# Causal attention with split-precision scores: the row sums of the last three key tiles of a chunk move from TensorE to VectorE, masks are merged, and visits to the values hold up to eight key tiles

## The chip, the cores and the metric

One core of one Trainium2 chip runs the whole program. The metric is the device time of that core in microseconds (us). The kernel before took 3632.71 us, the median of three runs (3631.72 to 3634.29).

## What is computed

A causal attention with grouped heads, a residual and a layer norm, then a linear layer with eight low-rank experts and a second layer norm. The change touches the attention alone:

```
q = (x @ wq).reshape(b, s, 32, 32)        # b = 2, s = 2048, x: [2, 2048, 1024]
k, v = (x @ wk), (x @ wv)                 # 8 key/value heads of 32, each shared by 4 query heads
scores = einsum('bihd,bjhd->bhij', q, k) * 32 ** -0.5
scores = where(causal, scores, min)
attn = softmax(scores, axis=-1)
out = einsum('bhij,bjhd->bihd', attn, v) @ wo
```

## The kernel before

The program has three stages, one behind the other: `project_qkv` (to about 550 us), `attend` (to about 2690 us) and `feed_forward`. The change lies in `attend`.

`attend` works on 16 groups, one for each batch and key/value head, with the group's four query heads side by side. For a group it does two things on TensorE (PE), interleaved:

- **The maxima.** Scores are computed with queries on the partitions, in *items* of up to 512 columns (`item`, L532), into a ring of three banks `qm`. VectorE (DVE) reduces each item to one maximum per row (L674) and so frees its bank. Diagonal items get a causal mask by a small matmul with the identity (L535). There are 140 such items in a group, and four transposes of the maxima (L524). They are computed half a group ahead of their use, and a table places two items (transposes counted) behind each step: 144 on 72 steps.
- **The exponentials and the values.** Scores are computed again with keys on the partitions (`scores`, L556, and L550 for the last tile), 128 keys by 256 queries by four heads in a pair of banks `km` (there are two pairs). ScalarE (ACT) takes the exponential (L637, and L634 for half a tile) into a ring of 18 tiles `probs`. Queries come in eight *chunks* of 256, numbered 0 to 7; chunk c has 2c + 2 key tiles, each a *step*, 72 in all. The last tile of a chunk is half masked away, and only 128 of its queries are computed.

Steps come in *slots* of at most five (`MOST = 5`), 18 slots in a group. Behind the scores of a slot TensorE makes a *visit* to the values (`values`, L566) for the slot before it: for each key tile four matmuls, one for each head in its own quarter of the array, multiply `probs` by `v` into `p2_o`. The profile counts each of these fp32 matmuls as two instructions, so that a tile shows as x8.

The denominators are the sums of `probs` over the keys. GpSimd (POOL) adds the first 2c - 1 tiles of chunks 2 to 7 into `psums` (L499 for the first pair, L503 for the rest), and one call of `weighted` multiplies the sum by ones. The last three tiles of these chunks, and all of chunks 0 and 1, are multiplied by ones on TensorE, tile by tile (`weighted(ones, probs)`, L566 too). In the last group POOL takes only c + 1 tiles of chunks 3 to 7 (`LAST_SUMS`). At the end of a chunk TensorE waits for POOL's last sum (`added`), and ACT copies `p2_o` out (L617).

Every engine works through its own list in order. SyncE issues all transfers. TensorE waits for ACT before it reuses a pair of `km`, for DVE before it reuses one of the three `qm` banks, for ACT's last exponential of a slot at the start of the visit to it, and for POOL at a chunk's end. ACT waits, before it overwrites a tile of the ring, for the visit and for POOL's sum that used it.

Of the kernel before, what the change touches and what calls it, by code (L numbers as in the profile page):

```python
# [5 lines left out]
F32 = mybir.dt.float32  # L6
# [8 lines left out]
P = 128  # L15
# [219 lines left out]
def attend(nc, sem, q_hi, q_lo, k_hi, k_lo, v_d, aT_d, den_d):  # L235
# [11 lines left out]
    MOST = 5  # L247
# [8 lines left out]
    PB = 18  # L256
    assert NS % PB == 0

# [4 lines left out]
    class Sums:  # L263

        def __init__(self, pooled):
            self.pooled = pooled
            self.adds_before = [sum(max(0, m - 1) for m in pooled[:c]) for c in range(NC + 1)]
            self.chunks = [sum(m > 0 for m in pooled[:c]) for c in range(NC + 1)]
# [4 lines left out]

        def adds_through(self, s):
# [5 lines left out]
    NADD, NCHUNK = SUMS.adds_before[NC], SUMS.chunks[NC]  # L280
# [59 lines left out]
    with ctx:  # L340
# [11 lines left out]
        psums = [sb(f"p2_psums{i}", [P, REP, CQ], F32) for i in range(2)]  # L352
        part_max = [sb(f"p2_part_max{c}", [P, REP, SUB, c + 1], F32) for c in range(NK)]
# [20 lines left out]
        added = sem("p2_added")  # L374
        chunk_done = sem("p2_chunk_done")
# [102 lines left out]
        def _(pool):  # L478
# [12 lines left out]
            def group(n, plan):  # L491
                for c in range(NC):
                    sums = psums[c % 2]
                    for t in range(1, plan.pooled[c]):
                        s = FIRST_STEP[c] + t
                        pool.wait_ge(exp_done, n * NS + s + 1)
                        if t == 1:
                            at_least(pool, chunk_done, n * NCHUNK + max(0, plan.chunks[c] - 1))
                            pool.tensor_tensor(sums[:, :, :], probs[(s - 1) % PB][:, :, :], probs[s % PB][:, :, :],  # L499
                                               ALU.add).then_inc(added, 1)  # L500
                        else:
                            pool.wait_ge(added, n * NADD + plan.adds_through(s) - 1)
                            pool.tensor_tensor(sums[:, :, :], sums[:, :, :], probs[s % PB][:, :, :],  # L503
                                               ALU.add).then_inc(added, 1)
# [7 lines left out]
        def _(pe):  # L512
            def item(m, par, i):
# [28 lines left out]
            def scores(n, par, s):  # L542
# [5 lines left out]
                if t == 2 * c + 1:  # L548
                    four = pair[:, 0, :].rearrange("p (h q) -> p h q", h=REP)
                    pe.matmul(four, keys, q_st[par][0:ROWS + 1, c // 2, :, q0 + P:q0 + CQ], start=True, stop=False)  # L550
                    last = pe.matmul(four, ident_bf[:, :], mask_k[:, :].unsqueeze(1).to_broadcast([P, REP, P]),
                                     start=False, stop=True)
                else:
                    for x in range(2):
                        two = pair[:, x, :].rearrange("p (h q) -> p h q", h=2)
                        last = pe.matmul(two, keys, q_st[par][0:ROWS + 1, c // 2, 2 * x:2 * x + 2, q0:q0 + CQ],  # L556
                                         start=True, stop=t < 2 * c)
                        if t == 2 * c:
                            last = pe.matmul(two[:, :, 0:P], ident_bf[:, :],
                                             mask_k[:, :].unsqueeze(1).to_broadcast([P, 2, P]), start=False, stop=True)  # L560
# [9 lines left out]
            def values(n, par, sl, plan):  # L570
# [7 lines left out]
                for s in steps:  # L578
                    t = STEPS[s][1]
                    last = weighted(v[par][:, t, :], probs[s % PB], 0, offset(s), t == 0)  # L580
                    if not plan.on_pool(s):
                        last = weighted(ones[:, :], probs[s % PB], CQ, offset(s), False)
                last.then_inc(slot_done, 1)
                if t == 2 * c + 1 and plan.pooled[c]:
                    pe.wait_ge(added, n * NADD + plan.adds_before[c + 1])
                    weighted(ones[:, :], psums[c % 2], CQ, 0, False).then_inc(chunk_done, 1)
# [23 lines left out]
        def _(act):  # L610
            def output(n, c, plan):
                if plan.pooled[c]:
# [13 lines left out]
            def exps(n, s, plan):  # L626
# [3 lines left out]
                if plan.on_pool(u % NS):  # L630
                    at_least(act, added, (n if u >= 0 else n - 1) * NADD + plan.adds_through(u % NS))
                act.wait_ge(scored, n * NS + s + 1)
                if offset(s):
                    act.activation(probs[s % PB][:, :, P:CQ], km[s % 2][:, 0, :].rearrange("p (h q) -> p h q", h=REP),  # L634
                                   ACT.Exp, scale=SCALE).then_inc(exp_done, 1)
                else:
                    act.activation(probs[s % PB][:, :, :].rearrange("p h q -> p (h q)"),  # L637
# [28 lines left out]
        def _(dve):  # L666
# [13 lines left out]
            def group(n, placed):  # L680
                for items in placed:
                    for ahead, i in items:
                        item(n + ahead, i)
# [8 lines left out]
            group(NG - 1, CLOSING)  # L692
# [746 lines left out]
```

## Time and profile before

| what | value |
|---|---|
| median of three runs | 3632.71 us |
| the profiled execution's own time | 3631.32 us |
| its span in the profile | 3629.2 us |
| mean granted TensorE clock | 0.986 |
| PE, PEld (weight loads), DVE, ACT, POOL busy | 97%, 68%, 53%, 41%, 43% |

The profile is of one execution; times in it count from the span's start. A matmul's start is measured, its end is modelled and overlaps the next one, so the pace of TensorE is read from starts and not from its busy share. A row of the timeline merges equal neighbours; the bracket at its end gives the engine's idle time before it, and who ended it.

### The profile page before, as it was taken

What the parts mean: (1) busy time and instruction counts of PE and PEld (TensorE: products, weight loads), DVE (VectorE), ACT (ScalarE), POOL (GpSimd) and SP (SyncE); (2) the same over time, 40 slices, a digit from 0 to 9 for tenths busy, and PEclk for the clock granted to TensorE, in tenths of its full rate; (3) what the DMA queues carried; (4) which work ended last, traced back from release to release, by engine and by line L of the source; (5) the groups of instructions that cost most, each with busy time, mean ns of one, the idle gap of its engine ahead of it and who ended that gap; (6) DMA issues with size and microseconds to landing.
All of it is one profiled execution on the core that took longest, in us unless ns stands there. A gap on an engine that the chain in (4) does not pass through costs nothing. (4 is left out here: it accounts for less than half of the span.)

```text
span 3629.2 us, 64158 instructions
## 1 busy us (share of the span) xinstructions
PE 3517.4 (97%) x26506; PEld 2460.0 (68%) x26506; DVE 1927.5 (53%) x3577; ACT 1491.4 (41%) x1839; POOL 1559.7 (43%) x672
## 2 busy tenths in 40 slices
PE   8999998999999999999999999999969999999999
PEld 7888885555565565665665556556537888888887
DVE  3121217666666666666666666666615666642223
ACT  3111112555555555555555555555542222221111
POOL 0000002767867777787786787787530000000000
PEclk9999997999999999999999999999989999999999
DMA  6343325021111111111112111110027777755553
GB/s 209 119 128 113 112 86 114 23 50 48 34 41 48 39 34 50 47 31 44 48 31 50 48 33 41 48 38 9 12 81 199 231 228 225 213 187 178 175 181 129
DMA packets 248227, 340.74 MB, mean 94 GB/s; under 512 B 55440, under 2 KB 150288, under 8 KB 247952
## 3 DMA queue, kind: packets, MB, share of 16 engines
q1 hardware_dynamic: 247952, 336.87, 31.6%
q8 instruction: 198, 3.24, 0.4%
q14 instruction: 77, 0.63, 0.1%
HBM read 203.08 MB, written 133.17 MB: 93 GB/s over the span
## 5 line engine op out<-in xcount | busy, mean ns | idle before, releaser
L674 DVE TENSOR_REDUCE p_part_max<-p_qm 128x1 f32<-128x512 f32 (+3 forms) x2240 | 1357.1, 669 | 716.5 <-PE p_qm L532 442.9
L503 POOL TENSOR_TENSOR p_psums<-p_psums,p_probs 128x1024 f32<-128x1024 f32 x560 | 1331.4, 2378 | 82.0 <-ACT p_probs L637 2.2
L637 ACT ACTIVATE p_probs<-p_km 128x1024 f32<-128x1024 f32 x1024 | 1032.0, 1024 | 542.5 <-PE p_km L556 438.1
L532 PE MATMUL p_qm<-p_k_st,p_q_st 96*128 96x512 f32 (+3 forms) x2560 | 916.4, 421 | 14.7 <-DMA p_q_st<-q_hi 10.7
L556 PE MATMUL p_km<-p_q_st,p_k_st 97*128 97x512 f32 x2048 | 714.5, 428 | 9.5 <-ACT p_probs L637 7.2
L532 PEld LDWEIGHTS p_qm<-p_k_st,p_q_st 96*128 96x128 f32 x2560 | 495.4, 196 | 230.8 <-DVE p_part_max L674 162.8
L566 PE MATMUL p_o<-p_probs,p_v 128*32 128x256 f32 (+1 forms) x9216 | 581.8, 371 | 0.0
L556 PEld LDWEIGHTS p_km<-p_q_st,p_k_st 97*128 97x128 f32 x2048 | 355.2, 192 | 156.3 <-issue 110.7
L499 POOL TENSOR_TENSOR p_psums<-p_probs 128x1024 f32<-128x1024 f32 x95 | 226.2, 2381 | 501.0 <-ACT p_probs L637 501.0
L566 PEld LDWEIGHTS p_o<-p_probs,p_v 128*32 128x32 f32 x9216 | 270.9, 110 | 213.6 <-issue 58.8
L41 PE MATMUL p_acc<-p_xT_hi,p_w_hi 128*128 128x512 f32 x640 | 250.1, 391 | 9.5 <-DVE p_w_lo L226 9.5
L42 PE MATMUL p_acc<-p_xT_lo,p_w_hi 128*128 128x512 f32 x640 | 249.8, 390 | 0.0
L43 PE MATMUL p_acc<-p_xT_hi,p_w_lo 128*128 128x512 f32 x640 | 249.7, 390 | 0.0
L214 DVE TENSOR_TENSOR p_out_lo<-p_acc,p_out_hi 128x512 fp32r<-128x512 f32 x80 | 55.3, 692 | 348.4 <-ACT p_out_hi L188 348.3
L41 PE MATMUL p_acc<-p_wo_hi,p_a_hi 128*128 128x512 f32 x512 | 209.1, 408 | 31.5 <-DVE p_a_lo L1219 31.5
L32 POOL MEMSET p_ident<- 128x128 f32 x2 | 0.4, 204 | 553.2 <-POOLq L63 542.0
L535 PE MATMUL p_qm<-p_mask_q,p_ident_bf 128*128 128x128 bf16 x1024 | 233.1, 236 | 0.0
L617 ACT ACTIVATE p_o_raw<-p_o 128x512 f32<-128x512 f32 x128 | 76.6, 599 | 367.5 <-PE p_o L566 367.5
L188 ACT ACTIVATE p_out_hi<-p_acc 128x512 fp32r<-128x512 f32 x80 | 47.9, 598 | 422.0 <-PE p_acc L43 408.5
L566 PE MATMUL p_o<-p_probs,p_ones 128*32 128x256 f32 (+1 forms) x3216 | 220.9, 346 | 0.0
L43 PE MATMUL p_acc<-p_wo_hi,p_a_lo 128*128 128x512 f32 x512 | 203.2, 397 | 0.0
L42 PE MATMUL p_acc<-p_wo_lo,p_a_hi 128*128 128x512 f32 x512 | 202.4, 395 | 0.0
(152 smaller groups left out, 3958.3 us busy)
## 6 DMA issues: line engine op xcount, KB each, us to landing
p_q_st<-q_hi SPq DMA_DIRECT2D x128, 256.0 KB, 4.7
p_x_raw<-in_xT SPq DMA_DIRECT2D x64, 256.0 KB, 3.5
q_hi<-p_out_hi SPq DMA_DIRECT2D x64, 256.0 KB, 2.0
q_lo<-p_out_lo SPq DMA_DIRECT2D x64, 256.0 KB, 2.3
p_q_st<-q_lo SPq DMA_DIRECT2D x64, 256.0 KB, 4.4
attended_T<-p_o_raw SPq DMA_DIRECT2D x128, 128.0 KB
p_a_raw<-attended_T SPq DMA_DIRECT2D x32, 512.0 KB, 4.9
p_recip<-reciprocals SPq DMA_DIRECT2D x128, 128.0 KB, 6.7
```

Source lines behind the costliest of these rows:

```text
L41: pe.matmul(out, lhs_hi, rhs_hi, start=first, stop=False)
L42: pe.matmul(out, lhs_hi, rhs_lo, start=False, stop=False)
L43: return pe.matmul(out, lhs_lo, rhs_hi, start=False, stop=last)
L499: pool.tensor_tensor(sums[:, :, :], probs[(s - 1) % PB][:, :, :], probs[s % PB][:, :, :], ALU.add).then_inc(added, 1)
L503: pool.tensor_tensor(sums[:, :, :], sums[:, :, :], probs[s % PB][:, :, :], ALU.add).then_inc(added, 1)
L532: last = pe.matmul(bank[:, x * keys:(x + 1) * keys], q_st[par][0:ROWS, c, h + x, sub * P:(sub + 1) * P], k_st[par][0:ROWS, j * CK:j * CK + ...
L535: last = pe.matmul(bank[:, (x + 1) * keys - P:(x + 1) * keys], ident_bf[:, :], mask_q[:, :], start=False, stop=True)
L556: last = pe.matmul(two, keys, q_st[par][0:ROWS + 1, c // 2, 2 * x:2 * x + 2, q0:q0 + CQ], start=True, stop=t < 2 * c)
L566: last = pe.matmul(o_ps[h * HD:(h + 1) * HD, at + o:at + CQ], lhs, rhs[:, h, o:CQ], start=first, stop=False, skip_group_check=True)
L617: act.activation(o_raw[c % 2][:, :], o_ps[:, :], ACT.Copy).then_inc(o_read, 1)
L637: act.activation(probs[s % PB][:, :, :].rearrange("p h q -> p (h q)"), km[s % 2][:, :, :].rearrange("p a b -> p (a b)"), ACT.Exp, scale=SC ...
L674: dve.reduce_max(part_max[c][:, h:h + heads, sub, j], qm[bank_of(i)][:, 0:item_width(i)].rearrange("p (h k) -> p h k", h=heads), AX.X).the ...
```

## The change

- **Visits.** `MOST` goes from 5 to 8 and the ring of `probs` from 18 to 22 tiles. A group has 12 slots instead of 18: chunks 0 to 3 have one each (2, 4, 6 and 8 steps), chunks 4 to 7 two each (of 5, 6, 7 and 8). The ring is no longer a divisor of 72, so its index runs on over the groups.
- **Row sums.** In chunks 2 to 7 VectorE adds the last three tiles into a new tile `vsums` (two buffers): one add of two whole tiles, then one add of half a tile. It does so behind the items of the chunk's last slot. TensorE multiplies each `vsums` by ones once, behind `psums`; the matmuls of the three tiles with ones are gone. In the last group VectorE takes all that POOL doesn't, in chunks 1 to 7. POOL's own share stays as it was.
- **Masks.** An item with several heads gets one mask matmul over a strided view of its bank, instead of one for each head. With keys on the partitions, the first diagonal tile is computed by halves of the queries, four heads at a time, and masked once with 512 columns instead of twice with 256. The columns computed stay the same.

```diff
-    MOST = 5
+    MOST = 8
-    PB = 18
+    PB = 22
...
-    SUMS = Sums([2 * c - 1 if c > 1 else 0 for c in range(NC)])
-    LAST_SUMS = Sums([c + 1 if c > 2 else 0 for c in range(NC)])
+    SUMS = Sums([2 * c - 1 if c > 1 else 0 for c in range(NC)], [2 * c - 1 if c > 1 else 2 * c + 2 for c in range(NC)])
+    LAST_POOLED = [c + 1 if c > 2 else 0 for c in range(NC)]
+    LAST_SUMS = Sums(LAST_POOLED, [m if c > 0 else 2 * c + 2 for c, m in enumerate(LAST_POOLED)])
...
@@ item (TensorE)
-                for x in range(item_heads(i)):
+                for x in range(heads):
                     last = pe.matmul(bank[:, x * keys:(x + 1) * keys], q_st[par][0:ROWS, c, h + x, sub * P:(sub + 1) * P],
-                                     k_st[par][0:ROWS, j * CK:j * CK + keys], start=True, stop=j < c)
-                    if j == c:
-                        last = pe.matmul(bank[:, (x + 1) * keys - P:(x + 1) * keys], ident_bf[:, :], mask_q[:, :],
-                                         start=False, stop=True)
+                                     k_st[par][0:ROWS, j * CK:j * CK + keys], start=x == 0, stop=j < c)
+                if j == c:
+                    diagonal = bank[:, 0:heads * keys].rearrange("p (h k) -> p h k", h=heads)[:, :, keys - P:keys]
+                    last = pe.matmul(diagonal, ident_bf[:, :], mask_q[:, :].unsqueeze(1).to_broadcast([P, heads, P]),
+                                     start=False, stop=True)
...
@@ values (TensorE)
-                    if not plan.on_pool(s):
-                        last = weighted(ones[:, :], probs[s % PB], CQ, offset(s), False)
+                    if not plan.on_pool(s) and not plan.on_vector(s):
+                        last = weighted(ones[:, :], probs[(n * NS + s) % PB], CQ, offset(s), False)
...
+                if t == 2 * c + 1 and plan.summed(c):
+                    pe.wait_ge(own_added, n * NOWN + plan.own_before[c + 1])
+                    weighted(ones[:, :], vsums[c % 2], CQ, 0, False).then_inc(chunk_done, 1)
...
@@ VectorE
+            def add(n, s, plan):
+                c, t = STEPS[s]
+                sums, o = vsums[c % 2], offset(s)
+                dve.wait_ge(exp_done, n * NS + s + 1)
+                if t == plan.first[c] + 1:
+                    at_least(dve, chunk_done, n * NCHUNK + max(0, plan.chunks[c] - 1))
+                    dve.tensor_tensor(sums[:, :, :], probs[(n * NS + s - 1) % PB][:, :, :], probs[(n * NS + s) % PB][:, :, :],
+                                      ALU.add).then_inc(own_added, 1)
+                else:
+                    dve.wait_ge(own_added, n * NOWN + plan.own_through(s) - 1)
+                    dve.tensor_tensor(sums[:, :, o:CQ], sums[:, :, o:CQ], probs[(n * NS + s) % PB][:, :, o:CQ],
+                                      ALU.add).then_inc(own_added, 1)
...
+            def group(n, placed, plan=SUMS):
+                for c, steps in SLOTS:
+                    for s in steps:
+                        for ahead, i in placed[s]:
+                            item(n + ahead, i)
+                    for s in steps:
+                        if STEPS[s][1] > plan.first[c]:
+                            add(n, s, plan)
```

ACT waits for `own_added` too before it overwrites a tile of the ring that VectorE adds.

How the order of instructions changes is seen at two places. The first is VectorE's list, in a group of the middle. Before, it holds reduces alone (x8 is eight in a row):

```order
L674 TENSOR_REDUCE p_part_max<-p_qm 128x1 x32
L678 TENSOR_REDUCE p_row_max<-p_part_max 128x16
L674 TENSOR_REDUCE p_part_max<-p_qm 128x4
L674 TENSOR_REDUCE p_part_max<-p_qm 128x2 x2
L674 TENSOR_REDUCE p_part_max<-p_qm 128x1 x8
```

And now, the same place, from the adds of chunk 4 to those of chunk 5:

```order
L714 TENSOR_TENSOR p_vsums<-p_probs 128x1024
L718 TENSOR_TENSOR p_vsums<-p_vsums,p_probs 128x4x128
L701 TENSOR_REDUCE p_part_max<-p_qm 128x1 x11
L705 TENSOR_REDUCE p_row_max<-p_part_max 128x16
L701 TENSOR_REDUCE p_part_max<-p_qm 128x4
L701 TENSOR_REDUCE p_part_max<-p_qm 128x2 x2
L701 TENSOR_REDUCE p_part_max<-p_qm 128x1 x8
L705 TENSOR_REDUCE p_row_max<-p_part_max 128x16
L701 TENSOR_REDUCE p_part_max<-p_qm 128x1
L714 TENSOR_TENSOR p_vsums<-p_probs 128x1024
L718 TENSOR_TENSOR p_vsums<-p_vsums,p_probs 128x4x128
```

Two adds now stand between the last reduce of a chunk and the first reduce of the next one.

The second place is TensorE's visit at a chunk's end, here that of chunk 7. Before, it is the last of four visits to that chunk, with four key tiles:

```order
L566 MATMUL p_o<-p_probs,p_v 32x256 x8
L566 MATMUL p_o<-p_probs,p_ones 32x256 x4
L566 MATMUL p_o<-p_probs,p_v 32x256 x4
L566 MATMUL p_o<-p_probs,p_ones 32x256 x4
L566 MATMUL p_o<-p_probs,p_v 32x128 x4
L566 MATMUL p_o<-p_probs,p_ones 32x128 x4
L566 MATMUL p_o<-p_psums,p_ones 32x256 x4
```

And now, the second of two visits to it, with eight:

```order
L584 MATMUL p_o<-p_probs,p_v 32x256 x28
L584 MATMUL p_o<-p_probs,p_v 32x128 x4
L584 MATMUL p_o<-p_psums,p_ones 32x256 x4
L584 MATMUL p_o<-p_vsums,p_ones 32x256 x4
```

The three calls with ones on single tiles are gone, one on `vsums` has come, and the tiles of the visit before are in this one.

## Rows read from the trace of the kernel before

**Rows 1.** The page, busy time of each engine, and two lines of 40 slices.
```profile
PE 3517.4 (97%) x26506; PEld 2460.0 (68%) x26506; DVE 1927.5 (53%) x3577; ACT 1491.4 (41%) x1839; POOL 1559.7 (43%) x672
...
PE   8999998999999999999999999999969999999999
...
POOL 0000002767867777787786787787530000000000
```
**Rows 2.** Windows: groups 1 to 14 together, then the first group, then the last.
```profile
core 0: us, PE busy (x) PEld busy (x) DVE busy (x) ACT busy (x) POOL busy (x), PEclk, DMA share, GB/s
...
731.51:2561.88 1830.37, 1798.91 (x16861) 1092.03 (x16857) 1195.24 (x2016) 1039.02 (x1176) 1395.67 (x588) 1.00 0.16 40
550.00:731.50 181.50, 175.25 (x1271) 104.02 (x1271) 127.32 (x216) 75.50 (x85) 96.07 (x41) 0.87 0.27 63
2561.88:2690.00 128.12, 118.61 (x1225) 67.38 (x1225) 43.04 (x72) 72.69 (x82) 65.35 (x28) 0.99 0.03 10
```
**Rows 3.** Timeline of PE, chunk 7 into the next group: start, us, engine, line, what.
```profile
1757.51 0.23 PE L532 MATMUL p_qm<-p_k_st,p_q_st 96*128 96x128 f32 x1
...
1758.18 0.48 PE L532 MATMUL p_qm<-p_k_st,p_q_st 96*128 96x512 f32 x1
...
1763.84 0.74 PE L556 MATMUL p_km<-p_q_st,p_k_st 97*128 97x512 f32 x2
...
1768.61 1.93 PE L566 MATMUL p_o<-p_probs,p_v 128*32 128x256 f32 x32
1770.48 0.73 PE L556 MATMUL p_km<-p_q_st,p_k_st 97*128 97x512 f32 x2
...
1780.22 0.61 PE L566 MATMUL p_o<-p_probs,p_ones 128*32 128x256 f32 x8
1780.65 0.61 PE L566 MATMUL p_o<-p_probs,p_v 128*32 128x256 f32 x8
...
1781.52 0.40 PE L566 MATMUL p_o<-p_probs,p_v 128*32 128x128 f32 x8
1781.73 0.40 PE L566 MATMUL p_o<-p_probs,p_ones 128*32 128x128 f32 x8
1783.21 0.64 PE L566 MATMUL p_o<-p_psums,p_ones 128*32 128x256 f32 x8 [1.07 <-POOL p_psums L503]
```
**Rows 4.** Timeline of DVE in the same stretch: two slots of chunk 7.
```profile
1764.86 5.07 DVE L674 TENSOR_REDUCE p_part_max<-p_qm 128x1 f32<-128x512 f32 x8 [1.57 <-PE p_qm L532]
1771.48 4.54 DVE L674 TENSOR_REDUCE p_part_max<-p_qm 128x1 f32<-128x512 f32 x8 [1.56 <-PE p_qm L532]
```
**Rows 5.** Waits from 1300 to 2200 us: who for whom, us in total, times, longest.
```profile
PEld p_qm L532 <- DVE p_part_max L674: 64.5, 191, 0.4
```
**Rows 6.** Timeline of POOL: chunks 5, 6 and 7 of one group.
```profile
1707.14 17.49 POOL L503 TENSOR_TENSOR p_psums<-p_psums,p_probs 128x1024 f32<-128x1024 f32 x7
1727.97 2.38 POOL L499 TENSOR_TENSOR p_psums<-p_probs 128x1024 f32<-128x1024 f32 x1 [3.35 <-ACT p_probs L637]
1730.50 22.56 POOL L503 TENSOR_TENSOR p_psums<-p_psums,p_probs 128x1024 f32<-128x1024 f32 x9
1753.03 2.38 POOL L499 TENSOR_TENSOR p_psums<-p_probs 128x1024 f32<-128x1024 f32 x1
1755.55 27.61 POOL L503 TENSOR_TENSOR p_psums<-p_psums,p_probs 128x1024 f32<-128x1024 f32 x11
```
**Rows 7.** Groups by line and shape, whole span: count, busy us, mean ns, idle before.
```profile
L206 DVE TENSOR_TENSOR p_xT_lo<-p_x_raw,p_xT_hi 128x512 fp32r<-128x512 f32 x64 | 43.7, 682 | 4.6 <-ACT p_xT_hi L181 4.6
...
L1215 DVE TENSOR_TENSOR p_a_raw<-p_a_raw,p_recip 128x1024 f32<-128x1024 f32 x32 | 39.2, 1224 | 72.4 <-DMA p_recip<-reciprocals 72.4
...
L1241 DVE TENSOR_TENSOR p_y<-p_acc,p_x 128x1024 f32<-128x1024 f32 x32 | 39.1, 1223 | 51.4 <-issue 46.1 <-PE p_acc L43 5.0
```
**Rows 8.** The page, its group of POOL's adds.
```profile
L503 POOL TENSOR_TENSOR p_psums<-p_psums,p_probs 128x1024 f32<-128x1024 f32 x560 | 1331.4, 2378 | 82.0 <-ACT p_probs L637 2.2
```
**Rows 9.** Timeline of PE in the last group, where no items are left.
```profile
2666.13 0.73 PE L556 MATMUL p_km<-p_q_st,p_k_st 97*128 97x512 f32 x2 [0.71 <-ACT p_probs L637]
```

More of the change, by code:

```diff
@@ L263, in attend, with __init__ @@
     class Sums:
[L265 to L268, printed above, removed]
+        def __init__(self, pooled, first):
+            self.pooled, self.first = pooled, first
+            adds = [max(0, m - 1) for m in pooled]
+            own = [max(0, 2 * c + 1 - m) for c, m in enumerate(first)]
+            self.adds_before = [sum(adds[:c]) for c in range(NC + 1)]
+            self.own_before = [sum(own[:c]) for c in range(NC + 1)]
+            self.chunks = [sum(m > 0 for m in own[:c]) for c in range(NC + 1)]
         def on_pool(self, s):
@@ L272, in on_pool, with on_vector @@
             return t < self.pooled[c]
+        def on_vector(self, s):
+            c, t = STEPS[s]
+            return t >= self.first[c]
         def adds_through(self, s):
@@ L352, in attend @@
         psums = [sb(f"p2_psums{i}", [P, REP, CQ], F32) for i in range(2)]
+        vsums = [sb(f"p2_vsums{i}", [P, REP, CQ], F32) for i in range(2)]
         part_max = [sb(f"p2_part_max{c}", [P, REP, SUB, c + 1], F32) for c in range(NK)]
@@ L547, in scores @@
                 keys, q0, pair = k_st[par][0:ROWS + 1, t * P:(t + 1) * P], (c % 2) * CQ, km[s % 2]
-                if t == 2 * c + 1:
-                    four = pair[:, 0, :].rearrange("p (h q) -> p h q", h=REP)
-                    pe.matmul(four, keys, q_st[par][0:ROWS + 1, c // 2, :, q0 + P:q0 + CQ], start=True, stop=False)
+                if t >= 2 * c:
+                    first = t - 2 * c
+                    for x in range(1, first - 1, -1):
+                        four = pair[:, x, :].rearrange("p (h q) -> p h q", h=REP)
+                        last = pe.matmul(four, keys, q_st[par][0:ROWS + 1, c // 2, :, q0 + x * P:q0 + (x + 1) * P],
+                                         start=True, stop=x > first)
                     last = pe.matmul(four, ident_bf[:, :], mask_k[:, :].unsqueeze(1).to_broadcast([P, REP, P]),
@@ L556, in scores @@
                         last = pe.matmul(two, keys, q_st[par][0:ROWS + 1, c // 2, 2 * x:2 * x + 2, q0:q0 + CQ],
[L557 to L560, printed above, removed]
+                                         start=True, stop=True)
                 last.then_inc(scored, 1)
@@ L678, in item @@
                     dve.reduce_max(row_max[c][:, :], part_max[c][:, :, :, :].rearrange("p h s j -> p (h s) j"), AX.X).then_inc(max_done, 1)
[L680 to L683, printed above, removed]
+            def add(n, s, plan):
+                c, t = STEPS[s]
+                sums, o = vsums[c % 2], offset(s)
[16 more added lines that the diff above has]
+                            add(n, s, plan)
             for i in range(2):
@@ L691, in _ @@
                 group(n, STEADY)
-            group(NG - 1, CLOSING)
+            group(NG - 1, CLOSING, LAST_SUMS)
 class Chain:
```

32 lines of the change are left out of this document (22 added, 10 removed).

## The prediction

> **What bounds the kernel now.** I read the shares and slices first: TensorE is busy 97% of the span, but its ends are modelled, so that says only that it has work or a modelled tail nearly always; POOL works in the attention alone [rows 1]. Then the windows: the 14 groups of the middle take 1830.37 us, 130.74 us each, at a clock of 1.00, and the first and last group are of the same size [rows 2]. So the question is what ends last inside one middle group, and that is in the timelines and the waits.
>
> A group is a row of score stretches and visits. *Visits run at TensorE's own pace.* A call over one whole tile starts 0.43 us after the one before (1780.22, 1780.65), over half a tile 0.21 us; a visit of four tiles lasts 1.87 us (1768.61 to 1770.48) [rows 3], that is 4 x 0.43 and 0.15 for the seam. *Score stretches are set by VectorE.* Its first reduce starts 1.02 us into a stretch (1763.84 to 1764.86), it then needs 0.634 us for each of eight items, and it is done 1.32 us after the visit has begun (1768.61 to 1769.93) [rows 3, 4]. TensorE, at most three banks ahead, waits for it 191 times in 900 us, 64.5 us in all [rows 5], 9.4 us a group. In a visit VectorE therefore idles for the visit's length less 0.3 us; the row gives 1.56 us for a visit of 1.87 [rows 4]. *POOL is the third bound, in the last two chunks.* Chunk 6's first add starts at 1727.97, and from there 22 adds run without a gap to 1783.16, 2.51 us each [rows 6]. TensorE, which is through with its tiles at 1781.94, has to wait for that last add: 1.27 us, of which the bracket shows 1.07 [rows 3]. From the start of chunk 6's adds to the end of the group, the chain is POOL's 55.2 us.
>
> **The change part by part**, for a middle group, on the profiled execution.
>
> 1. *Ones calls.* Six chunks lose 2.5 units each (a unit is a call over a whole tile) and gain one for `vsums`: 15 - 6 = 9 units, 9 x 0.43 = 3.87 us of visits less.
> 2. *Six visits fewer*, with the same tiles. TensorE saves six seams, 0.9 us. But VectorE loses its lead of 0.3 us of catching up at each, which stretches the score stretches by 6 x 0.31 = 1.86 us. Net +0.96 us: between -0.9 (if VectorE does not bind) and +1.7 (if all three banks count, 3 x 0.634 - 1.47 = 0.43 us a seam).
> 3. *Masks.* An item of four heads takes TensorE 0.67 us (1757.51 to 1758.18) against 0.235 for a plain one [rows 3]. Merging takes 320 mask matmuls of 1024 out of the program and 128 of the other kind. There are 4 such items a group and 8 with two heads, mostly where VectorE binds. I take 0.3 us, between 0 and 1.5.
> 4. *POOL's chain.* Of the parts above only what lies outside of chunks 6 and 7 counts, as POOL's 22 adds stay. TensorE's way over those two chunks took 54.0 us (1727.97 to 1781.94). It loses 7.5 units of ones and three seams (-3.7 us), and gains two calls on `vsums`, two tiles of chunk 5 that the visit at its end now holds, and 3 x 0.31 us (+2.6): about 53 us. So the wait for POOL grows from 1.27 to about 2.1 us. The group without any cost of the adds: 130.74 - 3.87 + 0.96 - 0.3 + (2.1 - 1.27) = 128.4 us, -2.4 us.
> 5. *The two adds of a chunk on VectorE.* Alone they take 1.224 us and, for the half tile, 0.682 us at most [rows 7]. They start when the reduces are done, 1.32 us into a visit; the next reduce is due 1.02 us behind the visit's end. The visit there is that of the slot before: 5 to 8 tiles, 2.3 to 3.6 us (chunks 2 and 3: 3.2 and 3.4). So 3.3 us have to fit into 3.3 to 4.6: alone they are hidden everywhere, with nothing to spare in chunk 4.
> 6. *The adds beside POOL.* In before no VectorE instruction with two tiles in SBUF runs while POOL adds, so the price has to be bounded. Low end: nothing. High end: they exclude each other, and each waits until the other's instruction is over. POOL's 2378 ns [rows 8] are 1.94 times VectorE's 1224 for the same add, as if it read its two tiles one behind the other, by one way in; VectorE's time is the same whether one input comes from PSUM or both from SBUF (1223 and 1224) [rows 7], so it reads two at a time. A second input in SBUF needs a way in of its own, and POOL's single way is the one candidate the rows suggest. I take the high end, without these rows proving it. The Trainium skill, SBUF — State Buffer, section Who interferes with whom, says so outright: VectorE's second SBUF input comes through the interface that it shares with GpSimd, and the later of the two instructions blocks until the other is done. No row here shows it.
>
> With exclusion, by chunk. In chunks 5, 6 and 7 POOL is busy without a gap when VectorE comes, so VectorE waits 1.2 us on average (half of 2.38). After its first add POOL has an add pending. If that goes first, the pair ends 1.32 + 1.2 + 1.22 + 0.13 + 2.38 + 0.69 = 6.9 us into the visit; if VectorE's second add goes first, at 4.5 us. The next reduce was due at 3.75 (chunk 5), 4.2 (6) and 4.6 (7). VectorE is late by 3.2, 2.8 and 2.3 us, or by 0.8, 0.3 and 0. Where VectorE binds, being late adds one for one. In chunks 3 and 4 POOL is in its last add: late by 0.3 and 1.1 us; in chunk 2 it is done. POOL in turn loses 1.95 us in each of chunks 6 and 7: its chain becomes 59.1 us. The lateness of chunk 5 falls behind chunk 6's first exponentials (three items are free), so it lies beside that chain: TensorE needs 53 + 3.2 + 2.8 + 2.1 = 61.1 us, or 54 with the kinder order. The rest of the group is 128.4 - 55.2 = 73.2 us, and 1.4 for chunks 3 and 4. So the group is 73.2 + 1.4 + 61.1 = 135.7 us, or 73.2 + 1.4 + 59.1 = 133.7: +5.0 or +3.0 us.
>
> *First and last group.* The first has more items and no wait for POOL: -3 us without exclusion, +3 with. In the last, TensorE loses 36.5 units and gains seven (-12.7 us), but VectorE takes 33 adds: chunks 1 to 4 have 3, 5, 3 and 4 in a row, 3.2 to 5.8 us that start 1.3 us into visits of 1.4 to 2.9 us, so about 9 us of reduces come late. Later there are no items, and ACT sets the stretches [rows 9]. -3 us, or +5 with exclusion (+1 with the kinder order). ACT's ring: a tile is reused 22 steps later instead of 18, with up to 16 tiles waiting for a visit; I see no stall and take 0. SyncE issues the same transfers, a few steps later or earlier, and its loads have half a group in hand: 0.
>
> **Sum.** With exclusion 14 x 5.0 + 8 = +78 us or 14 x 3.0 + 4 = +46 us; from 3631.3 us that is 3709 and 3677. Nothing shows which of the two goes first, so I take the middle: 3693 us. The profiled execution lies 1.4 us under the median, which I neglect.
>
> **The rivals.**
>
> *A. The adds run side by side* (faster). 14 x (-2.4) - 6 = -40 us: 3592 us, between 3570 (POOL's wait does not grow, masks give 1 us) and 3620. For it speaks that POOL's mean of 2378 ns is steady beside reduces that fill two thirds of the time. Against it, that these have one input, in PSUM. It decides by one number: if VectorE's pair takes under about 3 us in chunks 5 to 7, this is the case. It is against the skill's rule named above. Chance 0.36.
>
> *B. Only POOL pays* (slower, a little). VectorE never waits, or POOL's adds merely stretch: the chain is 59.1 us and nothing is late. 128.4 + 3.9 = 132.3, +1.6 us a group: 3655 us, 3625 to 3670. Chance 0.10.
>
> *C. The change saves nothing* because the ones calls filled time in which VectorE caught up: then item 1 is worth nothing where VectorE binds, since a shorter visit then only moves the time into the stretch. Against it: VectorE idles 1.56 us in a visit of 1.87, so visits are paid in full. With hidden adds: 3630 us. Chance 0.04.
>
> **How the numbers follow.** Forecast (exclusion, 3655 to 3730): 0.50. A 0.36, B 0.10, C 0.04. A change of 0.2% (7 us) is about what a measurement can tell from none. Faster: A and a little of B and C, 0.38. Same: 0.06. Slower: 0.56. The range has to reach from A to the forecast: 3585 to 3725 leaves out the better half-tail of A and the end beyond the worse order, some 0.2. The forecast's own range is 3655 to 3730.
>
> **What would show it.** Groups of the middle at 133.5 to 136 us. A new group of VectorE, `vsums`, with 96 first adds whose mean is well over 1.22 us or whose idle before is large; POOL's adds with gaps or a mean above 2378 ns where VectorE adds; the wait of TensorE for DVE well over 9.4 us a group. Visits: 12 a group, each 0.43 us a unit and 0.15. Wrong would be: VectorE's adds at 1.22 and 0.69 us and POOL's at 2378 with no gap between (then A), or a wait for POOL under 1 us a group (then item 4 is wrong).

## The result and the profile after

| | before | after |
|---|---|---|
| median of four runs | 3632.22 us | 3676.51 us |
| lowest and highest | 3631.15, 3634.29 | 3667.36, 3677.84 |
| ratio, with 95% interval | | 1.0113 [1.0099, 1.0128] |
| profiled execution: own time, span | 3631.32, 3629.2 us | 3667.36, 3665.2 us |
| mean granted TensorE clock | 0.986 | 0.961 |

The change makes the kernel 44 us slower. The profiled execution after is the lowest of its four, 9 us under their median; its span is 36.0 us longer than that of before, and that is what the rows below have to explain.

The page of the kernel after, lines that answer to [rows 1] and [rows 8], with the clock's slices:

```profile
PE 3477.1 (95%) x24354; PEld 2453.6 (67%) x24354; DVE 2277.8 (62%) x3790; ACT 1502.5 (41%) x1839; POOL 1606.3 (44%) x672
...
PEclk9999998999999999999999999999979999999999
...
L519 POOL TENSOR_TENSOR p_psums<-p_psums,p_probs 128x1024 f32<-128x1024 f32 x560 | 1373.0, 2452 | 96.1 <-ACT p_probs L664 19.4
...
L714 DVE TENSOR_TENSOR p_vsums<-p_probs 128x1024 f32<-128x1024 f32 x97 | 188.6, 1944 | 35.0 <-ACT p_probs L664 35.0
```

TensorE has 2152 instructions less and 40 us less of busy time, and yet ends later. VectorE has 350 us more. Its whole add takes 1944 ns on average, where the same shape took 1224 in the kernel before [rows 7], and POOL's add takes 2452 instead of 2378 ns for the same tiles.

**Where in the program.** Chunk by chunk, POOL's first add is a mark that both kernels have. Timeline of POOL before, at four marks: chunk 2 of groups 1 and 14, chunk 3 of the last group, and the first instruction behind the attention (the columns are those of [rows 6]).

```profile
746.26 2.38 POOL L499 TENSOR_TENSOR p_psums<-p_probs 128x1024 f32<-128x1024 f32 x1 [10.92 <-ACT p_probs L637]
...
2447.04 2.37 POOL L499 TENSOR_TENSOR p_psums<-p_probs 128x1024 f32<-128x1024 f32 x1 [9.78 <-ACT p_probs L637]
...
2591.07 2.39 POOL L499 TENSOR_TENSOR p_psums<-p_probs 128x1024 f32<-128x1024 f32 x1 [22.94 <-ACT p_probs L637]
...
2695.78 0.20 POOL L32 MEMSET p_ident<- 128x128 f32 x1 [11.23 <-POOLq L340]
```

And the same four after:

```profile
739.10 2.40 POOL L515 TENSOR_TENSOR p_psums<-p_probs 128x1024 f32<-128x1024 f32 x1 [10.19 <-ACT p_probs L664]
...
2469.40 2.40 POOL L515 TENSOR_TENSOR p_psums<-p_probs 128x1024 f32<-128x1024 f32 x1 [12.21 <-ACT p_probs L664]
...
2613.37 3.26 POOL L515 TENSOR_TENSOR p_psums<-p_probs 128x1024 f32<-128x1024 f32 x1 [23.30 <-ACT p_probs L664]
...
2731.53 0.21 POOL L32 MEMSET p_ident<- 128x128 f32 x1 [10.99 <-POOLq L354]
```

The differences are -7.2, +22.4, +22.3 and +35.8 us. So up to group 1 the change gains 7.2 us; the 13 periods from group 1 to group 14 lose 29.5 us, 2.3 us each (133.1 instead of 130.8 us); and the last group loses 13.4 us.

**What ends last in a middle group.** Waits from 1300 to 2200 us in the kernel after, to be laid beside [rows 5]:

```profile
PEld p_qm L549 <- DVE p_part_max L701: 70.9, 181, 1.2
...
PEld p_qm L540 <- DVE p_part_max L701: 46.3, 27, 3.3
```

The items' wait went from 64.5 to 70.9 us, no more. New is the second row: the transposes (L540) wait for a reduce, 46.3 us in seven groups and up to 3.3 us at once. They stand at the head of the score stretches behind the adds of chunks 5 and 6, where a reduce that comes late is met first. TensorE's wait for POOL's last add, 1.07 us a group before [rows 3], is at most 0.1 us a group in the same stretch.

**VectorE's adds one by one.** Timeline of DVE after, the pairs of chunks 2, 3, 5 and 6 of one group:

```profile
1542.42 1.21 DVE L714 TENSOR_TENSOR p_vsums<-p_probs 128x1024 f32<-128x1024 f32 x1
1543.74 0.69 DVE L718 TENSOR_TENSOR p_vsums<-p_vsums,p_probs 128x512 f32<-128x512 f32 x1
...
1555.34 3.36 DVE L714 TENSOR_TENSOR p_vsums<-p_probs 128x1024 f32<-128x1024 f32 x1
1558.80 0.69 DVE L718 TENSOR_TENSOR p_vsums<-p_vsums,p_probs 128x512 f32<-128x512 f32 x1
...
1596.09 1.56 DVE L714 TENSOR_TENSOR p_vsums<-p_probs 128x1024 f32<-128x1024 f32 x1
1597.75 2.69 DVE L718 TENSOR_TENSOR p_vsums<-p_vsums,p_probs 128x512 f32<-128x512 f32 x1
...
1621.02 3.18 DVE L714 TENSOR_TENSOR p_vsums<-p_probs 128x1024 f32<-128x1024 f32 x1
1624.31 2.66 DVE L718 TENSOR_TENSOR p_vsums<-p_vsums,p_probs 128x512 f32<-128x512 f32 x1
1626.89 3.16 DVE L701 TENSOR_REDUCE p_part_max<-p_qm 128x1 f32<-128x512 f32 x5
```

In chunk 2 POOL has nothing left to add, and the pair takes 1.21 and 0.69 us. In chunk 3 POOL is in its last add: the first add waits 2.15 us, inside its own recorded duration, and the second finds POOL idle. In chunks 5 and 6 POOL has a further add pending, and the second add takes 2.69 and 2.66 us, its own 0.69 and 2.0 more.

**What that does to TensorE.** Timeline of PE after, from the visit in which chunk 6's pair runs:

```profile
1619.77 3.23 PE L584 MATMUL p_o<-p_probs,p_v 128*32 128x256 f32 x56
1622.93 0.73 PE L577 MATMUL p_km<-p_q_st,p_k_st 97*128 97x512 f32 x2
1623.50 0.64 PE L549 MATMUL p_qm<-p_k_st,p_q_st 96*128 96x512 f32 x2
1623.97 0.63 PE L577 MATMUL p_km<-p_q_st,p_k_st 97*128 97x512 f32 x2
1624.44 0.40 PE L549 MATMUL p_qm<-p_k_st,p_q_st 96*128 96x512 f32 x1
1627.63 0.28 PE L540 MATMUL p_qm<-p_ident,p_row_max 128*16 128x128 f32 x1 [2.79 <-DVE p_part_max L701]
...
1629.16 0.86 PE L577 MATMUL p_km<-p_q_st,p_k_st 97*128 97x512 f32 x2
1629.82 1.05 PE L549 MATMUL p_qm<-p_k_st,p_q_st 96*128 96x512 f32 x2
1630.67 1.05 PE L577 MATMUL p_km<-p_q_st,p_k_st 97*128 97x512 f32 x2
```

The pair ends at 1626.97 (1624.31 and 2.66), 7.2 us into the visit. TensorE fills its three banks, waits 2.79 us for the first reduce behind the adds, and then goes on more slowly: two matmuls of 512 columns start 0.85 us before the next two (1629.82, 1630.67) instead of 0.47 (1623.50, 1623.97). The windows tell why (us, then busy time and count by engine, granted clock, DMA share and GB/s):

```profile
1622.00:1626.00 4.00, 2.84 (x27) 1.59 (x19) 3.90 (x2) 1.97 (x2) 3.86 (x2) 1.00 0.00 0
1626.00:1630.00 4.00, 2.27 (x8) 1.49 (x9) 4.00 (x6) 1.29 (x2) 3.60 (x3) 0.92 0.01 2
1630.00:1634.00 4.00, 4.00 (x13) 3.24 (x12) 2.37 (x5) 2.05 (x2) 3.86 (x2) 0.50 0.16 49
1634.00:1638.00 4.00, 4.00 (x19) 2.73 (x21) 3.16 (x6) 2.90 (x3) 3.71 (x3) 0.72 0.01 4
```

After the wait the granted clock is 0.50, which is the level of 1.2 GHz instead of 2.4; by these windows it lasts from about 1629.4 to 1636.2, 7 us. Behind chunk 5's pair TensorE waits 1.60 us (to 1601.10), and there too the clock falls, for 3.4 us:

```profile
1602.00:1606.00 4.00, 4.00 (x15) 3.25 (x13) 2.81 (x5) 2.11 (x3) 3.63 (x3) 0.57 0.01 2
```

Over groups 1 to 14 of [rows 2] the clock was 1.00; in the same stretch of the kernel after (723 to 2586 us) it is 0.95.

**POOL's chain** in the same group, chunks 6 and 7, beside [rows 6]:

```profile
1600.48 2.36 POOL L515 TENSOR_TENSOR p_psums<-p_probs 128x1024 f32<-128x1024 f32 x1 [0.59 <-ACT p_probs L664]
1603.06 23.36 POOL L519 TENSOR_TENSOR p_psums<-p_psums,p_probs 128x1024 f32<-128x1024 f32 x9 [0.23 <-ACT p_probs L664]
1626.38 2.81 POOL L515 TENSOR_TENSOR p_psums<-p_probs 128x1024 f32<-128x1024 f32 x1
1629.60 28.67 POOL L519 TENSOR_TENSOR p_psums<-p_psums,p_probs 128x1024 f32<-128x1024 f32 x11 [0.40 <-ACT p_probs L664]
```

It runs from 1600.48 to 1658.27, 57.8 us instead of 55.2. TensorE asks for its end only at 1660.39, 2.1 us later, since it has itself become later.

**The last group.** Timeline of PE, its longest wait:

```profile
2617.83 0.80 PE L549 MATMUL p_qm<-p_k_st,p_q_st 96*128 96x512 f32 x1 [5.45 <-DVE p_part_max L701]
```

A second one of 4.52 us comes at 2654.36, both for reduces behind a row of VectorE's adds, and in the four microseconds behind the first (2618 to 2622) the granted clock is 0.50.

### The profile page after: what moved, and what is told of

The parts are those of the page before. It is cut to its first block and busy times, and to the rows that moved or that the text cites. A ratio compares the mean times of both kernels' runs of the same rounds, so it can differ in the third digit from the quotient of the medians.

```text
span 3665.2 us, 60274 instructions
## 1 busy us (share of the span) xinstructions
PE 3477.1 (95%) x24354; PEld 2453.6 (67%) x24354; DVE 2277.8 (62%) x3790; ACT 1502.5 (41%) x1839; POOL 1606.3 (44%) x672
## 5 line engine op out<-in xcount | busy, mean ns | idle before, releaser
L519 POOL TENSOR_TENSOR p_psums<-p_psums,p_probs 128x1024 f32<-128x1024 f32 x560 | 1373.0, 2452 | 96.1 <-ACT p_probs L664 19.4
L664 ACT ACTIVATE p_probs<-p_km 128x1024 f32<-128x1024 f32 x896 | 906.2, 1025 | 363.8 <-PE p_km L577 334.5
L549 PE MATMUL p_qm<-p_k_st,p_q_st 96*128 96x512 f32 (+3 forms) x2560 | 952.6, 440 | 42.4 <-DVE p_part_max L701 27.1
L549 PEld LDWEIGHTS p_qm<-p_k_st,p_q_st 96*128 96x128 f32 x2560 | 512.8, 207 | 281.3 <-DVE p_part_max L701 198.4
L577 PE MATMUL p_km<-p_q_st,p_k_st 97*128 97x512 f32 x1792 | 642.8, 442 | 6.7 <-ACT p_probs L664 6.2
L584 PE MATMUL p_o<-p_probs,p_v 128*32 128x256 f32 (+1 forms) x9216 | 530.0, 374 | 0.0
L584 PEld LDWEIGHTS p_o<-p_probs,p_v 128*32 128x32 f32 x9216 | 282.8, 111 | 217.2 <-issue 46.1
L577 PEld LDWEIGHTS p_km<-p_q_st,p_k_st 97*128 97x128 f32 x1792 | 334.7, 206 | 121.0 <-issue 66.2
L660 ACT ACTIVATE p_probs<-p_km 128x1024 f32<-128x1024 f32 (+1 forms) x256 | 203.0, 811 | 127.4 <-PE p_km L572 112.8
L714 DVE TENSOR_TENSOR p_vsums<-p_probs 128x1024 f32<-128x1024 f32 x97 | 188.6, 1944 | 35.0 <-ACT p_probs L664 35.0
```

Source lines behind the costliest of these rows:

```text
L519: pool.tensor_tensor(sums[:, :, :], sums[:, :, :], probs[(n * NS + s) % PB][:, :, :], ALU.add).then_inc(added, 1)
L584: last = pe.matmul(o_ps[h * HD:(h + 1) * HD, at + o:at + CQ], lhs, rhs[:, h, o:CQ], start=first, stop=False, skip_group_check=True)
L660: act.activation(tile[:, :, first * P:CQ].rearrange("p h (x q) -> p x h q", q=P), km[s % 2][:, first:2, :].rearrange("p x (h q) -> p x h q ...
L664: act.activation(tile[:, :, :].rearrange("p h q -> p (h q)"), km[s % 2][:, :, :].rearrange("p a b -> p (a b)"), ACT.Exp, scale=SCALE).then ...
L714: dve.tensor_tensor(sums[:, :, :], probs[(n * NS + s - 1) % PB][:, :, :], probs[(n * NS + s) % PB][:, :, :], ALU.add).then_inc(own_added, 1)
```

## The experiments

The theory after the result: VectorE's adds and POOL's exclude each other (while one runs, the other waits); the late reduces stop TensorE, and its clock falls. Rivals: the merged masks or the longer visits cost the time; or the adds do by their mere length. A second question came up on the way: what part POOL's chain plays when it does not show as a wait. Ratios are against the kernel before on the same chip; the medians of before were 3631.1 to 3632.1 us.

**The three parts of the change alone.** The kernel before with the merged masks only:

> The kernel before with the merged masks alone. All theories: a few us less, since 448 mask matmuls go but the score stretches are set by VectorE: 3628 us, between 3615 and 3633. If it were the masks that cost something (a strided view of a bank), the time would be above 3640.

It took 3620.34 us, 0.9968 [0.9957, 0.9980]. Its timeline of PE shows an item of four heads, mask included:

```profile
1534.32 0.56 PE L550 MATMUL p_qm<-p_k_st,p_q_st 96*128 96x128 f32 x4
1534.71 0.39 PE L554 MATMUL p_qm<-p_mask_q,p_ident_bf 128*128 128x512 bf16 x1
1534.76 0.58 PE L550 MATMUL p_qm<-p_k_st,p_q_st 96*128 96x512 f32 x1
```

0.44 us (1534.32 to 1534.76), where [rows 3] have 0.67. The merge saves 12 us in all, and not 4. Most of the surplus lies outside the middle groups (see below).

The kernel before with longer visits and the larger ring only:

```diff
-    MOST = 5
+    MOST = 8
-    PB = 18
+    PB = 22
```

> The kernel before with slots of up to eight steps and the ring of 22 alone: 12 visits a group, every sum as before. Theory (VectorE's adds and POOL's adds exclude each other, and that is the whole loss): 3632 us, +-10; a group costs about 1 us more in VectorE's lost catching up and less in the wait for POOL. Rival (the long visits and stretches are the loss: VectorE, with three banks, binds in stretches of eight steps): 3660 us or more.

3622.04 us, 0.9969 [0.9955, 0.9983]: it saves 10 us. Neither of the two costs the time, so this rival falls; the fourth run below, with both and without the adds, says the same.

The kernel before with VectorE's adds only (visits of at most five tiles, ring of 18, masks as they were):

```diff
-    SUMS = Sums([2 * c - 1 if c > 1 else 0 for c in range(NC)])
+    SUMS = Sums([2 * c - 1 if c > 1 else 0 for c in range(NC)], [2 * c - 1 if c > 1 else 2 * c + 2 for c in range(NC)])
```

> The kernel before with VectorE's adds alone: slots of up to five steps, ring of 18, masks as before. Theory: visits are shorter (1.9 to 2.3 us instead of 2.7 to 3.6 where the adds stand), so the adds reach further into the next stretch: slower than the full change, 3700 us, 3680 to 3730. Rival (long visits are the loss): the adds save TensorE 3.9 us a group, 3590 us.

3720.98 us, 1.0247 [1.0230, 1.0264]. The adds cost 89 us here, where the visits that should hide them are shorter.

The other way round, the whole change without the adds, the three tiles multiplied by ones as before:

```diff
-    SUMS = Sums([2 * c - 1 if c > 1 else 0 for c in range(NC)], [2 * c - 1 if c > 1 else 2 * c + 2 for c in range(NC)])
+    SUMS = Sums([2 * c - 1 if c > 1 else 0 for c in range(NC)], [2 * c + 2 for c in range(NC)])
-    LAST_SUMS = Sums(LAST_POOLED, [m if c > 0 else 2 * c + 2 for c, m in enumerate(LAST_POOLED)])
+    LAST_SUMS = Sums(LAST_POOLED, [2 * c + 2 for c in range(NC)])
```

> The full change without VectorE's adds: merged masks, eight key tiles a visit, ring of 22, the last three tiles of a chunk multiplied by ones on TensorE. Theory: 3625 us, +-10, so that the adds alone cost some 50 us. Rival (long visits are the loss): 3665 us or more, since TensorE gets its ones calls back too.

3617.50 us, 0.9958 [0.9942, 0.9975]. So the adds, with the ones calls that they save, cost 3676.5 - 3617.5 = 59 us.

**Is it their length, or what they meet?** Each add is replaced by a maximum over one of its tiles, of the same size, so with one input in SBUF. The sums of the last three tiles are left out; all waits, and the call on `vsums`, stay.

```diff
-                    dve.tensor_tensor(sums[:, :, :], probs[(n * NS + s - 1) % PB][:, :, :], probs[(n * NS + s) % PB][:, :, :],
-                                      ALU.add).then_inc(own_added, 1)
+                    dve.reduce_max(sums[:, 0, 0:1], probs[(n * NS + s) % PB][:, :, :].rearrange("p h q -> p (h q)"),
+                                   AX.X).then_inc(own_added, 1)
...
-                    dve.tensor_tensor(sums[:, :, o:CQ], sums[:, :, o:CQ], probs[(n * NS + s) % PB][:, :, o:CQ],
-                                      ALU.add).then_inc(own_added, 1)
+                    dve.reduce_max(sums[:, :, o:o + 1], probs[(n * NS + s) % PB][:, :, o:CQ], AX.X).then_inc(own_added, 1)
```

> The full change, but each of VectorE's adds is a maximum over the tile it would have added: the same place, the same waits, about the same length, but one input in SBUF instead of two. The sums of the last three tiles are left out of the denominators. Theory (two inputs in SBUF exclude POOL's adds): the instructions take about 1.1 and 0.6 us with no wait in them, no stretch starts late, and the clock stays at 0.98: 3590 us, 3575 to 3605. Rival (VectorE merely has too much work, or the wait on the exponentials holds it): as the full change, 3660 to 3680 us.

3643.96 us, 1.0031 [1.0019, 1.0043]. Groups by shape, 1300 to 2200 us:

```profile
L519 POOL TENSOR_TENSOR p_psums<-p_psums,p_probs 128x1024 f32<-128x1024 f32 x246 | 585.6, 2380 | 35.3
L714 DVE TENSOR_REDUCE p_vsums<-p_probs 128x1 f32<-128x1024 f32 x41 | 49.6, 1209 | 0.0
L718 DVE TENSOR_REDUCE p_vsums<-p_probs 128x4 f32<-128x512 f32 x41 | 28.2, 689 | 4.2
```

The instructions themselves behave as expected: 1209 and 689 ns on VectorE, 2380 on POOL, side by side, and no reduce is late. A maximum also writes one or four elements where the add writes its whole tile, so this run leaves open whether the second input or the large output makes the difference; no run here separates the two. The time does not come out as expected: 3590 was expected, and 54 us more were measured. What took them is in this kernel's waits and its timeline of PE:

```profile
PE p_o L584 <- POOL p_psums L519: 27.3, 7, 3.9
```

```profile
1517.04 1.08 PE L584 MATMUL p_o<-p_psums,p_ones 128*32 128x256 f32 x8 [3.90 <-POOL p_psums L519]
```

A TensorE that is not held up by VectorE reaches the end of chunk 7 before POOL, waits 3.9 us in each group, and the clock falls again. Windows of the same kernel, around and behind that row:

```profile
1518.00:1522.00 4.00, 4.00 (x19) 2.57 (x12) 1.29 (x2) 1.67 (x3) 0.00 (x0) 0.50 0.15 41
1522.00:1526.00 4.00, 4.00 (x13) 1.86 (x11) 2.46 (x4) 2.00 (x2) 0.00 (x0) 0.50 0.17 58
```

The same wait is not always followed by the same fall. Two neighbouring groups of this kernel, from mark to mark, each with one wait of 3.9 us:

```profile
1003.89:1136.86 132.97, 127.60 (x1081) 76.85 (x1080) 95.79 (x157) 74.47 (x86) 100.05 (x43) 0.95 0.16 41
1136.86:1266.74 129.88, 124.54 (x1081) 75.64 (x1080) 95.63 (x157) 74.59 (x86) 100.00 (x43) 0.97 0.16 42
```

Windows of 1 us show the lower clock for 13.7 us in the first and for 6.8 us in the second; the second is 3.1 us shorter. That is what 6.8 us of the lower clock cost here.

The other side of the pair, VectorE's adds whole and POOL's cut to 64 of 1024 columns (the rest of POOL's sums is left out):

```diff
-                            pool.tensor_tensor(sums[:, :, :], sums[:, :, :], probs[(n * NS + s) % PB][:, :, :],
+                            pool.tensor_tensor(sums[:, 0:1, 0:64], sums[:, 0:1, 0:64], probs[(n * NS + s) % PB][:, 0:1, 0:64],
```

> The full change, but POOL's adds cover 64 columns instead of 1024, so that POOL is idle nearly always; most of POOL's sums are left out of the denominators. Theory: VectorE's adds take 1.22 and 0.69 us everywhere, TensorE never waits for POOL: 3580 us. Rival (VectorE's adds are slow or late by themselves): 3660 us.

3536.63 us in a single run, 43 us less than expected. TensorE doesn't wait for POOL at all in it, and POOL has next to nothing to do, so its time holds more than the price of exclusion. Groups by shape, 1300 to 2200 us:

```profile
L716 DVE TENSOR_TENSOR p_vsums<-p_probs 128x1024 f32<-128x1024 f32 x43 | 52.3, 1216 | 0.0
L720 DVE TENSOR_TENSOR p_vsums<-p_vsums,p_probs 128x512 f32<-128x512 f32 x43 | 29.8, 693 | 4.5
```

VectorE's adds are back at 1216 and 693 ns. They lengthen only while POOL adds whole tiles, and POOL's adds only beside VectorE's adds, not beside the maxima of the same length. Their length alone makes no reduce late.

**Two chains: late reduces and POOL.** The change with VectorE's second add behind the items of the next slot, so that each of the two is alone:

```diff
+            waiting = []
...
+                    while waiting:
+                        add(*waiting.pop())
...
-                            add(n, s, plan)
+                            if plan is SUMS and STEPS[s][1] == 2 * c + 1:
+                                waiting.append((n, s, plan))
+                            else:
+                                add(n, s, plan)
```

> The full change, but the second add of a chunk stands behind the reduces of the next slot, so that each visit has one add to hide instead of two (3.7 and 3.2 us against visits of 2.7 to 3.6 us and 1.0 us more). Theory: both adds still wait for POOL, but hardly any stretch starts late and the clock stays up: 3620 us, 3605 to 3640. Rival (POOL's longer chain is the loss): no change against the full change, 3665 us or more.

3673.47 us, 1.0108 [1.0091, 1.0124]: a miss, nothing is gained. The late reduces are gone (the transposes wait 15.9 us in seven groups, 14.8 before), and in their place stands POOL:

```profile
PE p_o L584 <- POOL p_psums L519: 44.2, 7, 6.3
```

6.3 us a group, and the lower clock with it (from 1396 to 1403 us around the wait that ends at 1399.86). The change with POOL relieved alone, one tile less in chunk 6 and two in chunk 7, which TensorE multiplies by ones:

```diff
-    SUMS = Sums([2 * c - 1 if c > 1 else 0 for c in range(NC)], [2 * c - 1 if c > 1 else 2 * c + 2 for c in range(NC)])
+    SUMS = Sums([2 * c - 1 - {6: 1, 7: 2}.get(c, 0) if c > 1 else 0 for c in range(NC)], [2 * c - 1 if c > 1 else 2 * c + 2 for c in range(NC)])
```

> The full change with POOL's chain alone shortened: one tile less in chunk 6, two less in chunk 7, both of VectorE's adds where the change has them. Theory (in the full change the late reduces end last, and POOL's chain lies beside them): little comes back, 3660 us, 3645 to 3680, and the wait for the transpose stays. Rival (POOL's chain is the loss, and moving the second add was not needed): as with both, 3581 us.

3650.92 us (3636.66 to 3670.79), 1.0068 [1.0042, 1.0093]. The late reduces stay, the transposes wait 34.2 us (in the fastest of the five runs, the profiled one). The five runs differ by 34 us, and their mean clock goes with them: 0.973 in the fastest, 0.960 in the slowest. And both edits together:

> The full change with the second add behind the reduces of the next slot (3673 us before this), and POOL with one tile less in chunk 6 and two less in chunk 7. Theory (exclusion costs twice: it delays VectorE's reduces, or, where that is hidden, POOL's chain, and waits of over 3 us cost TensorE's clock): both are now out of the way: 3600 us, 3585 to 3620, clock 0.98. Rival (something else in VectorE's adds costs): 3650 us or more.

3580.79 us, 0.9862 [0.9845, 0.9880], 4 us below the expected range. In its 13 periods from group 1 to group 14, of 126.2 to 126.5 us each, the clock doesn't fall at all. Once more as a table:

| | POOL as in the change | POOL relieved |
|---|---|---|
| both adds in one place | 3677 | 3651 |
| second add a slot later | 3673 | 3581 |

One edit alone gives 3 or 26 us, both give 96. The two delays lie beside each other, and each hides most of the other. The same relief without any exclusion (maxima in place of the adds, the last three tiles' sums left out again):

> The maxima in place of VectorE's adds (one input in SBUF, 3644 us before this), with POOL's chain three tiles shorter as well. Theory (what was left of the loss was the wait for POOL of 3.9 us a group and the clock that it cost): 3575 us, 3560 to 3590, clock 0.98. Rival (VectorE's additional instructions cost by their length): 3620 us or more.

3557.16 us, 0.9790 [0.9770, 0.9810], 3 us below the expected range. So with POOL out of the way the exclusion costs 3651 - 3557 = 94 us where the adds stand together, and 3581 - 3557 = 24 us where they are apart.

**Adding where POOL's chain is not hit.** VectorE adds in chunks 2 to 4 only, and in chunks 6 and 7 of the last group; elsewhere TensorE multiplies by ones.

```diff
-    SUMS = Sums([2 * c - 1 if c > 1 else 0 for c in range(NC)], [2 * c - 1 if c > 1 else 2 * c + 2 for c in range(NC)])
+    SUMS = Sums([2 * c - 1 if c > 1 else 0 for c in range(NC)], [2 * c - 1 if 1 < c < 5 else 2 * c + 2 for c in range(NC)])
-    LAST_SUMS = Sums(LAST_POOLED, [m if c > 0 else 2 * c + 2 for c, m in enumerate(LAST_POOLED)])
+    LAST_SUMS = Sums(LAST_POOLED, [m if c > 5 else 2 * c + 2 for c, m in enumerate(LAST_POOLED)])
```

> The full change, but VectorE adds only in chunks 2, 3 and 4, where POOL is idle or in its last add when VectorE comes; in chunks 5 to 7 the last three tiles are multiplied by ones on TensorE as before. Theory: half of the saved calls without the lateness: 3612 us, 3600 to 3622. Rival (every add on VectorE costs): between 3617 us (no adds) and 3676 (all), about 3645 us.

3593.04 us, 0.9887 [0.9871, 0.9904], better than the expected range by 7 us. TensorE waits for POOL at most 1.6 us a group, and the clock over the middle groups rounds to 1.00: it falls in three groups, for 3.4 us each, and these take 129.4 to 129.5 us instead of 127.9. Last, the same with one tile less for POOL in chunk 7:

```diff
-    SUMS = Sums([2 * c - 1 if c > 1 else 0 for c in range(NC)], [2 * c - 1 if 1 < c < 5 else 2 * c + 2 for c in range(NC)])
+    SUMS = Sums([2 * c - 1 - {7: 1}.get(c, 0) if c > 1 else 0 for c in range(NC)], [2 * c - 1 if 1 < c < 5 else 2 * c + 2 for c in range(NC)])
```

> VectorE adds in chunks 2 to 4 alone (3593 us before this), and POOL gets one tile less in chunk 7, which TensorE multiplies by ones instead. Theory (POOL's chain over chunks 6 and 7 still ends last, with 1.6 us of wait a group): the chain loses 2.5 us, TensorE gains 0.43: -1.1 us a group, 3577 us, 3570 to 3588. Rival (POOL's wait is cover for TensorE and ends nothing): 3600 us.

3574.75 us, 0.9841 [0.9823, 0.9859]. This version computes everything and is 1.6% faster than the kernel before and 2.8% faster than the change. Groups of its profile, 1300 to 2200 us:

```profile
L520 POOL TENSOR_TENSOR p_psums<-p_psums,p_probs 128x1024 f32<-128x1024 f32 x250 | 594.9, 2380 | 35.8
L717 DVE TENSOR_TENSOR p_vsums<-p_probs 128x1024 f32<-128x1024 f32 x21 | 41.5, 1976 | 0.0
L721 DVE TENSOR_TENSOR p_vsums<-p_vsums,p_probs 128x512 f32<-128x512 f32 x21 | 14.5, 692 | 2.2
```

VectorE still waits in its first add (1976 ns on average), but its second finds POOL done, and POOL's long chain runs at 2380 ns.

## Why the prediction was right, and where it was not

The direction was right, and so was the first cause, exclusion: 3693 us was said and 3676.5 measured, inside the forecast's own range. The way from there to the time was not right in its parts. It is luck that the measured time lies within 1 us of 3677, the sum for the kinder order, for the order was the other one.

- *Item 6, exclusion: right.* The nearest rows only suggested it. Now 1.21 and 0.69 us stand beside 3.36 and 2.69 for the same instructions, and a VectorE instruction of the same length with one input in SBUF shows nothing of it. By the rule of the Trainium skill, SBUF — State Buffer, section Who interferes with whom, the trace agrees: two SBUF inputs on VectorE wait for POOL's instruction, one input does not. That it is the second input and not the large output is not shown by these runs.
- *Item 6, the order: right that it is one of the two, wrong to take the middle.* POOL's pending add went first in each pair of chunks 5 to 7 behind which POOL had one pending (second adds of 2.66 to 2.70 us). The pair ends 7.2 us into the visit in chunk 6, and 6.9 was said. In chunk 3 the pair ended 5.4 us into the visit (1554.12 to 1559.49), 1.0 us late with 0.3 said; in chunk 4 it was not late (an add of 1.40 us), with 1.1 said.
- *Item 6, the longer of two ways: the right shape, with wrong terms.* For the order that occurred the sum lets TensorE need 61.1 us over chunks 6 and 7 and POOL 59.1. (Its third lateness is 2.1 in the sum and 2.3 in the list before it, a slip of 0.2.) TensorE took 59.9 us (1600.48 to 1660.39), POOL 57.8. But the lateness was smaller, some 3.7 us of waits (the 0.6 left of chunk 5's 1.60, 2.79 and 0.26) where 8.1 was said, and the clock filled the gap.
- *Item 4 and its test.* The wait for POOL fell from 1.07 us a group to at most 0.1, which the prediction names as a sign that item 4 is wrong. That sign didn't fit its own sum: where TensorE's way is the longer one, no such wait is left. What tests item 4 is the kernel with nothing late (one input): there TensorE is through 51.4 us after chunk 6's first add (1461.76 to 1513.14), where 53 was said, and waits 3.9 us, where 2.1 was said.
- *Item 2, fewer visits: the wrong sign.* +0.96 us a group was said. Alone, with the marks used above, the middle groups take 129.68 us instead of 130.83: -1.15, a little beyond the lower bound of -0.9. The last group loses 7.2 us instead, so that only 10 remain in all. Why VectorE's catching up at a seam costs so little was not followed further.
- *Item 3, masks: about right where it was meant.* 0.3 us a group was said, and the middle groups are 0.4 shorter (130.44); 4.4 of the 12 us come before group 1, which the item doesn't treat. In three of the 13 periods the lower clock takes 1.4 us back. With both parts the middle groups take 129.41 us, -1.4, nearly the sum of the two.
- *First and last group: a fair sum of two wrong terms.* Up to group 1 -7.2 us (+3 said), last +13.4 (+5 said): waits of 5.45 and 4.52 us and the clock behind them.
- *Not foreseen at all: the clock.* The prediction took waits as lost time only. In the group shown TensorE has the lower clock for 3.4 us behind the wait of 1.60 and for 7 us behind that of 2.79. Its way over chunks 6 and 7 is 59.9 us, 51.4 with nothing late, and 3.7 of the difference are waits: the clock costs the rest, some 5 us (an estimate). Not all of that could come back, since POOL's last add ends only 2.1 us before TensorE asks for it.
- *Rival A was priced too low.* With the exclusion taken away the change gives 3644 us and not 3592, because the wait for POOL, and the clock, come instead. By that kernel a version side by side would have been 12 us slower than before, not 40 faster.

A middle group came out at 133.1 us, +2.3, with 133.7 and 135.7 said. The total is near the forecast because terms cancel: the savings of items 2 and 3 (1.4 us a group together, where a cost of 0.7 was said) and the smaller lateness bring it down, and the clock brings it up.

## What to carry to other kernels

Before work moves to VectorE beside a busy POOL, look at how many of its inputs are in SBUF: with two, each instruction waits for POOL's current one and POOL for it, so put such work where POOL is idle, one instruction at a time, and not between two reduces that another engine needs. When two delays lie beside each other, an experiment that removes one of them can show next to nothing (3 us here, against 96 for both); before it is given up, ask which wait has taken the place. And a short wait of TensorE can cost more than its length, where the clock falls behind it.

## What the runs showed of the hardware

- VectorE's wait for POOL is recorded inside the duration of its own instruction, not as idle time before it: it shows as a mean above the known duration of the shape (1944 against 1224 ns).
- Between two VectorE adds, 0.1 us apart, a POOL add that was pending got in each time, so the second one paid 2.0 us.
- POOL loses less than VectorE's adds last: its chain of 22 adds grew by 2.6 us, beside four VectorE adds in chunks 6 and 7 that need 3.8 us alone.
- Behind a wait of 2.79 us in an otherwise busy TensorE the granted clock was 0.50 for 7 us, and from within waits of 3.90 us on for 7 or 14; behind one of 1.60 us it was 0.50 for 3.4 us. The falls are not tied to the length of a wait alone: in the kernel that adds in chunks 2 to 4 only, each of the 14 groups has a wait for POOL of 1.5 to 1.6 us and one for the maxima of 1.3 to 1.4 us, and three groups show a fall of 3.4 us, one behind the first wait (988.37 us) and two behind the second (1174.15 and 1303.69 us). The kernel before has waits of 1.1 us and no fall in these groups. What tells these apart stays open.
- One mask matmul of 512 columns over a strided bank, instead of four of 128, takes an item of four heads from 0.67 to 0.44 us.
